# One PSUM buffer or two for the V projection of an eight-core transformer layer

## The reference

```python
q = jnp.einsum('bsd,hde->bhse', x, wq) + bq        # x is the layer-normed input
k = jnp.einsum('bsd,hde->bhse', x, wk) + bk
v = jnp.einsum('bsd,hde->bhse', x, wv) + bv
scores = jax.nn.softmax(jnp.einsum('bhse,bhte->bhst', q, k) * scale, axis=-1)
att = jnp.einsum('bhst,bhte->bhse', scores, v)     # then heads side by side, @ wo.T + bo
# h = silu(x w1 s1) * (x w2 s2); h = gelu(h h1 sh1); h = gelu(h h2 sh2); out = h w3 s3
x = x + attention(layernorm(x))
x = x + ffn(layernorm(x))
```

## Time and profile before

| | us |
|---|---|
| runs of before | 3710.2 and 4256.6, median 3983.4 |
| profiled execution | 3710.27 |
| its span, slowest core (core 0) | 3708.7 |
| spans of the eight cores | 3696.4 to 3708.7 |
| TensorE busy | 3308.9 (89%) |
| ScalarE busy | 801.9 (22%) |
| VectorE busy | 485.9 (13%) |

### The profile page before, as it was taken

How to read it: one execution, slowest core, us unless ns; L and a number is a source line. 1 busy time by engine, 2 the same in 40 slices (tenths; PEclk the granted TensorE clock), 3 DMA queues, 4 the chain that set the end, 5 groups by cost and what they waited for, 6 DMA issues and landing times.

```text
span 3708.7 us, 34874 instructions; the slowest of 8 cores (3696.4 to 3708.7 us)
## 1 busy us (share of the span) xinstructions
PE 3308.9 (89%) x14422; PEld 1369.4 (37%) x14676; DVE 485.9 (13%) x491; ACT 801.9 (22%) x740; POOL 152.5 (4%) x291
## 2 busy tenths in 40 slices
PE   2367888888867799999999999999999999999999
PEld 0122222222212244444444444444444444444444
DVE  0533222222142503000000000000300000000000
ACT  1103777777831120000000000003000000000000
POOL 0000000000000011000000000001100000000000
PEclk9698999999978799999999999999999999999999
DMA  7000000001005255444444444455554444444444
GB/s 159 0 0 1 1 1 1 1 1 23 1 35 156 40 75 90 78 80 73 75 80 74 75 80 78 93 126 77 74 97 72 79 73 78 76 80 73 75 83 128
DMA packets 49613, 237.41 MB, mean 64 GB/s; under 512 B 7777, under 2 KB 7842, under 8 KB 28338
## 3 DMA queue, kind: packets, MB, share of 16 engines
q0 software_dynamic: 40208, 193.08, 30.8%
q1 hardware_dynamic: 9250, 42.08, 3.3%
HBM read 411.19 MB, written 16.78 MB: 115 GB/s over the span
## 4 chain that ended last, share of the span: by engine, by line
PE 65%; DMA 1%; DVE 1%; issue 0%; ACT 0%; DVEq 0%; ACTq 0%; POOLq 0%
PE ps_f L1141 65%; DVE act_bf L194 1%; DMA wb<-h 1%; PE ps_r L1065 0%; PE ps_m L1061 0%; ACT hbufA L1165 0%; DMA wb<-w 0%; DVE ostg L1192 0%; ACT hbufB L1165 0%; DVEq L193 0%; ACTq L1157 0%; POOLq L1106 0%; DVEq L1191 0%; DVEq L1189 0%; DVEq L1179 0%
## 5 line engine op out<-in xcount | busy, mean ns | idle before, releaser
L1141 PE MATMUL ps_f<-hbufB,wb 128*128 128x512 bf16 x5018 | 1102.0, 379 | 15.5 <-DMA wb<-h 7.1
L1141 PE MATMUL ps_f<-hbufA,wb 128*128 128x512 bf16 x4014 | 880.1, 379 | 7.2 <-ACT hbufA L1165 2.9
L1141 PEld LDWEIGHTS ps_f<-hbufB,wb 128*128 128x128 bf16 x5120 | 501.1, 98 | 616.4 <-issue 14.3
L1141 PEld LDWEIGHTS ps_f<-hbufA,wb 128*128 128x128 bf16 x4096 | 400.6, 98 | 486.7 <-issue 3.9
L820 ACT ACTIVATE pbuf<-ps_sc,cneg 128x1024 bf16<-128x1024 f32 x512 | 529.2, 1134 | 196.5 <-PE ps_sc L435 195.0
L1141 PE MATMUL ps_f<-act_bf,wb 128*128 128x512 bf16 x2006 | 448.9, 383 | 21.5 <-DVE act_bf L194 14.7
L1141 PEld LDWEIGHTS ps_f<-act_bf,wb 128*128 128x128 bf16 x2048 | 200.7, 98 | 271.8 <-issue 35.6
L456 PE MATMUL ps_aE<-pbuf,vt_sb 128*65 128x512 bf16 x512 | 220.4, 430 | 86.2 <-DVE q_sb L804 85.7
L1192 DVE SCALAR_TENSOR_TENSOR ostg<-ps_f,s_sb,x2rb 128x1024 f32<-128x1024 f32 x16 | 20.5, 1284 | 1984.5 <-PE ps_f L1141 1984.5
L1165 ACT ACTIVATE hbufB<-ps_f,sh_sb 128x1024 bf16<-128x1024 f32 x64 | 71.3, 1114 | 816.0 <-PE ps_f L1141 816.0
L1165 ACT ACTIVATE hbufA<-ps_f,sh_sb 128x1024 bf16<-128x1024 f32 x64 | 71.4, 1115 | 784.8 <-PE ps_f L1141 784.7
(11 more groups left out here) (96 smaller groups left out, 930.8 us busy)
## 6 DMA issues: line engine op xcount, KB each, us to landing
wb<-h POOLq DMA_DIRECT2D x128, 1024.0 KB, 8.0
wb<-w POOLq DMA_DIRECT2D x128, 256.0 KB, 3.8
wb<-w POOLq DMA_DIRECT2D x16, 1024.0 KB, 8.9
xrb<-xst SPq DMA_DIRECT2D x8, 1024.0 KB, 4.7
x2hbm<-x2buf SPq DMA_DIRECT2D x8, 1024.0 KB, 15.6
x2rb<-x2hbm SPq DMA_DIRECT2D x16, 512.0 KB, 9.2
out_fm<-ostg SPq DMA_DIRECT2D x16, 512.0 KB, 8.5
wqld<-wq POOLq DMA_DIRECT2D x1, 2048.0 KB, 16.1
```

Source lines behind the costliest of these rows:

```text
L1141: ins = t.matmul(ps_f[:, (i % 2) * 1024 + nn * 512:(i % 2) * 1024 + (nn + 1) * 512], wb[i % 3][:, k * 128:(k + 1) * 128], rhs[:, k * rstri ...
```

## The change

V chunks no longer go to `ps_x`. A new `emit_vchunk2` writes the two halves of `ps_sc` in turn, and waits before chunk c for the fence of chunk c - 2 (`s_vt`). V chunks no longer count as uses of `ps_x`; their eviction reads the half of `ps_sc` and counts on VectorE's own semaphore `s_v` instead of `s_xe`. The order of the instructions on each engine stays.

```diff
+                def emit_vchunk2(t, c):
+                    if c >= 2:
+                        t.wait_ge(s_vt, c - 1)
+                    ins = None
+                    for k in range(KD):
+                        for nn in range(2):
+                            ins = t.matmul(
+                                ps_sc[:, (c % 2) * 1024 + nn * 512:
+                                      (c % 2) * 1024 + (nn + 1) * 512],
+                                act_bf[:, k * S + c * 128: k * S + (c + 1) * 128],
+                                wv_sb[:, k * 1024 + nn * 512: k * 1024 + (nn + 1) * 512],
+                                start=(k == 0), stop=(k == KD - 1))
+                    ins.then_inc(s_pe, 1)
+                    n["pe"] += 1
+                    vch_pe[c] = n["pe"]
+
                 def emit_vt_evac(v, c):
                     v.wait_ge(s_pe, vch_pe[c])
                     v.wait_ge(s_v, n["v"])
                     v.tensor_add(
                         vt3[:, c * 16:(c + 1) * 16, 0:64],
-                        ps_x[:].rearrange("p (h e) -> p h e", e=64),
+                        ps_sc[:, (c % 2) * 1024:(c % 2) * 1024 + 1024]
+                        .rearrange("p (h e) -> p h e", e=64),
                         bvrep_sb.rearrange("p (h e) -> p h e", e=64)
-                    ).then_inc(s_xe, 1)
-                    xu["xe"] += 1
-                    v.wait_ge(s_xe, xu["xe"])
+                    ).then_inc(s_v, 1)
+                    n["v"] += 1
+                    v.wait_ge(s_v, n["v"])
                     if c >= 1:
                         v.wait_ge(s_vt, c)
-                    v.wait_ge(s_v, n["v"])
                     v.tensor_copy(
                         fence_vt, vt_sb[0:1, c * 16 * 65: c * 16 * 65 + 1]
                     ).then_inc(s_vt, 1)
@@ three places that emit chunks 0 to 6, 7, and 8 to 15
-                        emit_vchunk(t, c)
+                        emit_vchunk2(t, c)
-                    emit_vchunk(t, KD - 1)
+                    emit_vchunk2(t, KD - 1)
-                        emit_vchunk(t, c)
+                        emit_vchunk2(t, c)
```

## The result

The changed kernel takes 3683.4 us (median of 12 executions) where the kernel before takes 3713.0 (median of 11, taken beside it). The ratio is 0.9912, with a 95% interval from 0.9892 to 0.9933: 0.9% faster, which is clear of zero and under the 2% of a verdict. The ratio agrees with the times only if it counts an execution of before of 3739.4 us; without that one it would be 0.992, and 28.7 us between the medians. The forecast was 3681.

The account below looks back on a forecast made before the run. TensorE was taken to idle at V-stage handoffs, waiting for VectorE's evictions of `ps_x`. Savings of 23.9 + 3.5 + 1.7 = 29.2 us from 3710.3 gave 3681 us, likeliest case 3669 to 3693, full range 3665 to 3702.

Parts of the forecast that it names:

- The pitch: V chunks start 3.45 us apart instead of 5.16, taken from the FFN's w1 matmuls at 0.2158 us each.
- The spare time: VectorE needs 1.54 us per V chunk within two pitches, 6.9 us, so the new wait has about 5 us to spare.
- The handoffs: Waits removed in the V stage: 14 chunk to chunk, 23.9 us, and 2 from K to first chunk, 3.5 us.
- The row on the path: Replicated row after chunk 7 starts 1.71 us sooner; chunk 7's eviction ends 1.4 us ahead of it, so all counts.
- What stays: Multiplies, chunk 15's eviction and squares keep their lengths; attention and FFN only start sooner, lengths within some 10 us.
- The granted clock: Left out of the sum: clock luck in stalls after the change, up to 12 us either way, 3669 to 3693 us.
- rival 3: Denser matmuls lower the granted clock in V chunks 0 to 15: 26.7 us more, 3737 us; chance 0.05.
- Rival 1: Eviction and matmuls disturb each other in PSUM; only 8 us gained over 17 handoffs, 3702 us; chance 0.04.
- Rival 2: No effect: another wait ends where the removed one did, or the gain is lost later; 3710 us; chance 0.05.
- The rule against it: Skill page's kernel gained nothing further from PSUM double-buffering (126.6 to 125.5 us); by it about 0, 3710 us; small chance.

Follow-up runs that it names:

- the second half alone: Changed kernel, but V chunks 0 to 7 stay in `ps_x` with the old eviction and only 8 to 15 use `ps_sc`; one execution, 3698.3 us.
- one buffer: Changed kernel, but all V chunks go to the same half of `ps_sc`, each behind the last one's fence; ratio to before 0.9981 (0.9963 to 0.9999).

## Why the prediction was right

- *The pitch.* 3.45 us from the FFN's rows; measured 3.45 between evictions. It is the same loop shape on the same kind of buffers, in the same kernel, and that made it exact.
- *The spare time was misread.* The prediction gave VectorE two pitches, 6.9 us, for its 1.54 us and found 5 us to spare. But VectorE can begin on a chunk only behind its 3.6 us of matmuls, so what is left is 1.57 us (the fence of chunk 1 ends at 201.93, chunk 3 begins at 203.50). The new wait costs nothing, as forecast, but with a third of the margin claimed, and with the eviction doubled only 0.24 us of it are left.
- *The handoffs.* 14 of 1.71, 2 of 1.77 and the row's 1.71, in sum 29.2 us. The first scores moved by 30.6 us in the mean of the cores. The kernel with the second half alone and the one with one buffer show the parts. The excess of 1.4 us was in no term of the sum. The traces have three gains behind it, all at places where the granted clock changes. The row took 1.98 us instead of 2.17 to 2.73: its granted clock is 1.00 (220.8 to 222.8 us, core 3), where it was 0.76 before (235.6 to 238.1 us, core 0); from the row to Q of the second half this is 0.5 us. Q of the second half, to the start of K, took 0.7 us less in the mean (6.5 to 6.8 us on seven cores, 7.3 to 7.8 before). K of the second half took 3.61 us on all eight cores, where three cores had 5.30 before, 0.6 us in the mean; on core 3 its granted clock was 0.68 (256.2 to 261.5 us). Of these 1.8 us some 0.4 are lost again in small pieces (the first Q, the norms, the start of the stage). The prediction had filed the third under luck. Whether it was luck or came with the change, one trace of before can't tell; the changed kernel has 3.61 us on all cores in its second trace too.
- *The row on the path.* The eviction of chunk 7 (221.11, fence to 222.65) was over 0.9 us ahead of the memset (223.57), so the row did set the end; the margin was less than the 1.4 us of the prediction since the row is shorter.
- *What stays.* Attention and the stages behind it changed by +1.5, -0.4 and +1.7 us in the mean, within the 10 us allowed. They took back about 3 of 30.6.
- *The granted clock.* The sum had no term for it and a range of 12 us either way. The slowest core of the profiled execution gained 26.4 us, the medians differ by 28.7 to 29.6: the middle held. That 3683.4 lies within 3 us of 3681 is in part luck, as 1.4 us more at the first scores and 2.8 us given back behind them nearly cancel. The bound of 12 us, read off one execution's cores, was wider than what two measurements of the same kernel show (2 us).
- *A slip in rival 3.* For a loss of over 2% (74 us), 26.7 of them in V, the low level must stay for another 95 us of dense work by the prediction's own rule, and not 97. Nothing hangs on it.
- *Rival 1* (disturbance) fell with the evictions, still 1.23 us, and the chunks, 3.45 us apart, and again with the doubled eviction. *Rival 2* (no effect) fell with the times; its counter-argument, a fence 5 us early, should have read 1.57. *Rival 3* (a lower clock in V) didn't happen: the window from 195 to 220 us has TensorE busy throughout and a granted clock of 1.00.

```profile
195.00:220.00 25.00, 25.00 (x118) 11.32 (x116) 9.58 (x14) 0.00 (x0) 0.00 (x0) 1.00 0.00 1
```

The doubled eviction in the kernel before showed the opposite: there the granted clock fell when TensorE idled more, not when it worked more. The Trainium skill's account, page "TensorE: Matmul & The Clock Gate", section "A second HAM failure mode: psum-queue depth-cycling", that idling between groups of matmuls makes the clock swing between its two levels, agrees with that run (0.57 over the slow chunk) and not with the V chunks of the kernel before, where TensorE idles 1.55 us at each handoff and the granted clock stays at 1.00.
- *The rule against it.* The Trainium skill, page "TensorE: Matmul & The Clock Gate", section "HAM oscillation — how this bites in real kernels", has a kernel in which double-buffering PSUM gave no further gain. That doesn't carry over: it gave 29 us here, where the trace had the wait in it.

## What to carry to other kernels

Where one buffer passes between two engines and both wait in turn, a second buffer saves, per handoff, the whole difference between the old pitch and the larger of the two engines' times, as long as one group's matmuls, the start of the eviction and the eviction together fit in two pitches (5.3 of 6.9 us here). A loop of the same shape elsewhere in the trace, already double-buffered, gives the new pitch (here to 0.01 us). Count the neighbours of the loop too, since the uses of the old buffer ahead of it and behind it stop waiting as well, and look whether the slack of the faster engine can take the serial work that stands beside the loop: here that was worth another 30 us, as much as the change itself. When small differences are read off single traces, compare from the start of the changed stage: here that point alone moved by 1 us between traces.

## What the runs showed of the hardware

- With 1.55 us idle in each 5.16 us, TensorE's granted clock was 1.00 over the V chunks. With 1.86 us in each 5.47 (the one-buffer kernel) the chunks took 3.61 us too, but for chunk 9 on three cores, behind 2.24 us idle, which took 5.3. With 2.88 us idle in each 6.49 it fell for single chunks (4.9 to 6.6 us instead of 3.61, granted 0.57 over one). So a stall on the path cost over a quarter more than its own length: 27 us for 21.
- A granted clock of 0.81 showed in the output projection of cores 0 and 1 in the profile of the changed kernel with the eviction doubled; the other six cores had 0.93 to 0.99 there. The Trainium skill, page "TensorE: Matmul & The Clock Gate", section "Seeing it yourself", has 13/16 of the clock as a current limit, of a whole die. The level agrees; that only two cores of the die showed it does not. What set it off stays open. Executions of the kernel before have pairs of cores with the same mean clock and about 10 us more, but none of them has a trace that shows where.
- The stages behind the change lengthen and shorten by some microseconds with the moment at which they begin: attention took 735.8 us in the mean from a start at 319.2 us, 737.3 from 288.6, 739.6 from 273.0, and 735.9 from 258.7. The changes of the granted clock within it may be the cause; no run here isolates them.
